# Strip attention: maxima and exponentials of two heads in one instruction over two PSUM banks

## Chip, cores, metric

One NeuronCore of a Trainium2 chip runs the whole program in one launch. The metric is the device time in microseconds (us) of an execution; the median over several runs is compared.

## What is computed

The input is an image batch of shape (2, 96, 256, 256). One layer normalises it over channels, runs windowed attention, a convolutional MLP on the map, adds the result to the input, and ends with a quantised feed-forward. The part that the change touches is the attention over overlapping windows of 16 x 16 pixels, 14 apart:

```python
tok = crop.transpose(0, 2, 3, 4, 5, 1).reshape(b * n, ps * ps, c)
y = _layernorm(tok, norm1_w, norm1_b)
q = (y @ wq).reshape(b * n, ps * ps, HEADS, hd_q).transpose(0, 2, 1, 3)
k = (y @ wk).reshape(b * n, ps * ps, HEADS, hd_q).transpose(0, 2, 1, 3)
v = (y @ wv).reshape(b * n, ps * ps, HEADS, hd_v).transpose(0, 2, 1, 3)
scores = jnp.einsum('bhnd,bhmd->bhnm', q, k) / jnp.sqrt(jnp.float32(hd_q))
attn = jax.nn.softmax(scores, axis=-1)
out = jnp.einsum('bhnm,bhmd->bhnd', attn, v)
tok = out @ wproj + tok
```

There are 4 heads, 256 tokens a window, 16 query and 24 value channels a head, and 2 x 19 x 19 = 722 windows. Their outputs are added where windows overlap, with weights.

## The kernel before

Three stages run one after another: `norm_stage`, `attention_stage` and `map_stage`. Each writes its result to HBM. Only `attention_stage` is touched. It goes through 38 strips of 16 rows (19 per image), and through 19 windows in each strip. Here they are counted from zero, windows 0 to 18, and strips as first, second, ... in order of time: "strip 11" is the eleventh, and its window 0 begins at 1901.98 us of the trace. A window begins where its transposes (L652) begin.

Every engine has its own program for the stage, written out for the 19 windows of a strip (`body`), and a hardware loop that holds two strips. The order on each engine is the order of the code; engines wait for each other by semaphores that count. What TensorE does for window j, in this order:

- `maxima` (L652): two transposes that turn the row maxima NM of window j into a row, in bank 0 (`B_MT`). It waits for all maxima of window j (L679) and for the exponential of head 0 of window j - 1 (L681), which read bank 0.
- `scores` of window j + 1, heads 0 and 1 (L645), in bf16, into banks 4 and 5. They are only there for the row maxima.
- in 16 of the 19 windows a query/key product of 512 tokens of a strip (`queries_keys`, L624, which waits for Y from GpSimd) or a projection (`project`, L632, which waits for GpSimd's sums), by the tables `QK_STEP` and `OUT_STEP`. Windows 9, 11 and 13 have none.
- `scores_t` (L660): the transposed scores of all four heads of window j in fp32, into banks 0 to 3. It waits for VectorE's query row QF (L696) and for the exponentials of window j - 1.
- `scores` of window j + 1, heads 2 and 3 (L645), into the same banks 4 and 5 as heads 0 and 1; so it waits for the maxima of heads 0 and 1 of window j + 1 (L701).
- `weigh` (L668) for window j - 1 and `values` (L636) for window j + 1.

VectorE makes for window j the query row QF from the transposed maxima (`query_row`, L806), then the four row maxima of window j + 1 (`row_max`, L812), then what the tables put there: `residual` (L830), `queries16` (L797), the reciprocals and shares of the softmax sums (`shares`, L820 and L824) and `keys16` (L801). ScalarE makes `keep_qk` (L737), the four exponentials of window j (L759) into PROB, then copies the values (L741) and the output of window j - 1 (L749).

SP moves the keys to their own tensor (L386), gathers the softmax sums of a group of windows (L394), stores their reciprocals (L401) and spreads them back (L405). GpSimd weighs the group's outputs and adds them up (L543 to L559), and makes the next strip's normalised input Y (L496). `GROUPS` are the windows 0 to 4, 5 to 9, 10 to 14 and 15 to 18.

The banks are named in one line, and the two places where a pair of heads is handled are these:

```python
B_ST, B_S, B_MT, B_OV, B_CK = (0, 1, 2, 3), (4, 5, 4, 5), 0, 6, 7

for u in range(4):
    A.activation(PROB[:, par, u, :], P[:, B_ST[u], :], ACT.Exp, scale=DQ ** -0.5).then_inc(act_exp, 1)

for u in range(4):
    if u % 2 == 0:
        dve.wait_ge(pe_s, n(s, 2 * NPOS, 2 * j + u // 2 + 1))
    V_.tensor_reduce(NM[:, :, 32 * u + DQ], P[:, B_S[u], :].rearrange("p (a m) -> p a m", a=2),
                     axis=AX.X, op=ALU.max).then_inc(dve_max, 1)
```

Of the kernel before, what the change touches and what calls it, by code (L numbers as in the profile page):

```python
# [7 lines left out]
HEADS, DQ, DV = 4, 16, 24  # L8
MLP, FFN = 192, 384
PATCH, STEP = 16, 14  # L10
NPOS = 19
# [10 lines left out]
ALU, ACT, AX = mybir.AluOpType, mybir.ActivationFunctionType, mybir.AxisListType  # L22
# [231 lines left out]
def attention_stage(nc, xhat, rnorm, n1w, n1b, wq, wk, wv, wproj, ident, share, qrows, sums, x2map, nstrip=NSTRIP):  # L254

    ctx = ExitStack()
    with ctx:
        def sb(name, shape, dt=fp32):
            return ctx.enter_context(nc.sbuf_tensor(name, shape, dt))
# [28 lines left out]
        NM = sb("NM", [128, 2, 128])  # L288
        PROB = sb("PROB", [128, 2, 4, 2 * PT])
        P = ctx.enter_context(nc.psum_tensor("P1", [128, 8, 512], fp32))  # L290
        B_ST, B_S, B_MT, B_OV, B_CK = (0, 1, 2, 3), (4, 5, 4, 5), 0, 6, 7
# [16 lines left out]
        NWINS = nstrip * NPOS  # L308
# [299 lines left out]
        def _(pe):  # L608
# [40 lines left out]
            def maxima():  # L649

                for half in range(2):
                    m = T.transpose(P[:, B_MT, half * 128:half * 128 + 128], NM[:, half, :], IDN[:, :])  # L652
                m.then_inc(pe_mt, 1)
# [19 lines left out]
            def body(s, n, k, prev, follow):  # L673
                kept, outs = 2, -4
                for j in range(NPOS):
                    par = (s * NPOS + j) % 2
                    more = follow or j < LAST
                    nj = (j + 1) % NPOS
                    pe.wait_ge(dve_max, n(s, 4 * NPOS, 4 * j + 4))  # L679
                    if prev or j > 0:  # L680
                        pe.wait_ge(act_exp, n(s, 4 * NPOS, 4 * j - 3))  # L681
                    maxima()
                    if more:
                        pe.wait_ge(dve_kb, n(s, NCK, NCK * ((j + 1) // NPOS) + first_new(nj) + 1))
                        scores(nj, 0, 1)
                    for c, at in QK_STEP.items():
                        if at == j and (c > 1 or follow):
                            queries_keys(s + (c < 2), n, c, n(s, NCK, outs) if prev or outs > 0 else None)
                            kept += 1
                    for c, at in OUT_STEP.items():  # L690
                        if at == j and (c < 4 or prev):
                            project(s - (c > 3), n, c, n(s, NCK, kept), n(s, NCK, outs) if prev or outs > 0 else None)
                            outs += 1
                        elif at == j:
                            outs += 1
                    pe.wait_ge(dve_qf, n(s, NPOS, j + 1))  # L696
                    if prev or j > 0:
                        pe.wait_ge(act_exp, n(s, 4 * NPOS, 4 * j))
                    scores_t(j)
                    if more:  # L700
                        pe.wait_ge(dve_max, n(s, 4 * NPOS, 4 * j + 6))  # L701
                        scores(nj, 2, 3)
                    pe.wait_ge(act_v, n(s, NPOS, j + 1))
                    if prev or j > 1:
                        pe.wait_ge(act_os, n(s, NPOS, j - 1))
                    if prev or j > 0:
                        weigh(1 - par)
                    if more:
                        values(nj)
# [3 lines left out]
            queries_keys(0, n0, 1, None)  # L713
            pe.wait_ge(dve_kb, 1)
            scores(0, 0, 1)
            pe.wait_ge(dve_max, 2)
            scores(0, 2, 3)
            values(0)
            strips(pe, body)
            last = nstrip - 1  # L720
            pe.wait_ge(act_exp, 4 * NWINS)
            pe.wait_ge(act_os, NWINS - 1)
            pe.wait_ge(act_v, NWINS)
            weigh((NWINS - 1) % 2)
# [4 lines left out]
        def _(act):  # L729
            A = nc.scalar  # L730
# [20 lines left out]
            def body(s, n, k, prev, follow):  # L751
                for j in range(NPOS):
                    par = (s * NPOS + j) % 2
                    for c, at in QK_STEP.items():
                        if at == j and (c > 1 or follow):
                            keep_qk(s + (c < 2), n, c, not prev and c > 1)
                    act.wait_ge(pe_st, n(s, NPOS, j + 1))
                    for u in range(4):
                        A.activation(PROB[:, par, u, :], P[:, B_ST[u], :], ACT.Exp, scale=DQ ** -0.5).then_inc(act_exp, 1)  # L759
                    if follow or j < LAST:  # L760
                        keep_v(s, n, j + 1, 1 - par)
                    if prev and j == 0:
                        keep_o(s - 1, n, LAST, k is None and s == 1)
                    elif j > 0:
                        keep_o(s, n, j - 1, not prev)
# [9 lines left out]
        def _(dve):  # L775
            V_ = nc.vector
# [29 lines left out]
                V_.scalar_tensor_tensor(QF[:, :], QS[:, win(j)], MSK[:, 0:1], P[:, B_MT, 0:PT], ALU.mult, ALU.subtract).then_inc(dve_qf, 1)  # L806

            def row_max(s, n, j):
                for u in range(4):
                    if u % 2 == 0:  # L810
                        dve.wait_ge(pe_s, n(s, 2 * NPOS, 2 * j + u // 2 + 1))
                    V_.tensor_reduce(NM[:, :, 32 * u + DQ], P[:, B_S[u], :].rearrange("p (a m) -> p a m", a=2),  # L812
                                     axis=AX.X, op=ALU.max).then_inc(dve_max, 1)

            def shares(s, n, q, first):

# [850 lines left out]
```

## Time and profile before

| | |
|---|---|
| median of 3 runs | 9166.02 us (9153.25 to 9173.01) |
| profiled execution, its own time | 9185.78 us |
| its span, first to last instruction | 9184.0 us |
| TensorE busy (matmul) | 8035.3 us, 87% |
| VectorE busy | 5221.1 us, 57% |
| ScalarE busy | 4672.3 us, 51% |
| GpSimd busy | 2150.5 us, 23% |
| attention stage, by the windows' first and last transposes | about 957 to 4550 us |

Times of instructions come from the one profiled execution. Matmuls are pipelined and overlap in the records, so a busy TensorE isn't TensorE at its peak. In a row of the timeline, the first number is the start and the second the time to the end of the last of the xN instructions, all in us; what stands in brackets is how long the engine sat idle before it and what released it. PEld is TensorE's weight load, which runs ahead of the multiplications, so its wait alone is no idle time of the array.

### The profile page before, as it was taken

The page shows a single profiled execution, that of the slowest core. Times are in us where ns is not written, and L with a number is a line of the kernel's source. Part 1 is how long each engine was busy: PE and PEld are TensorE (multiplying, and loading weights), DVE is VectorE, ACT ScalarE, POOL GpSimd, SP SyncE. Part 2 cuts the span into 40 slices and gives each one's busy share as a digit, 9 for nine tenths or more (in the row PEclk, how much of TensorE's full clock was granted, in tenths as well). Part 3 has the DMA queues.
Part 4 walks back from the last instruction along what each step waited for, and adds up shares of the span by engine and source line. Part 5 has one row for each costly group of instructions (what it writes and reads, how often), then busy time and mean ns, then how long its engine had stood idle before and what let it go on. Part 6 is the DMA issues. An engine that isn't in the chain of part 4 may idle for free.

```text
span 9184.0 us, 208496 instructions
## 1 busy us (share of the span) xinstructions
PE 8035.3 (87%) x76932; PEld 4839.5 (53%) x76932; DVE 5221.1 (57%) x9929; ACT 4672.3 (51%) x8702; POOL 2150.5 (23%) x1712
## 2 busy tenths in 40 slices
PE   6776899999999999999858989989989888998998
PEld 3333444444444444444445566666666666666665
DVE  5565677777777777777633444444444444444444
ACT  2221555555555555555525555555555555555554
POOL 0000333333333333333301211212111121121111
PEclk8888899999999999999969999999999999999999
DMA  4333343333433334333251111111111111111110
GB/s 119 113 114 104 88 98 87 91 94 84 100 83 94 94 84 98 86 92 94 71 45 34 44 40 34 44 40 35 43 40 43 35 43 41 34 44 40 35 43 24
DMA packets 480819, 612.84 MB, mean 67 GB/s; under 512 B 173263, under 2 KB 415697, under 8 KB 455317
## 3 DMA queue, kind: packets, MB, share of 16 engines
q1 hardware_dynamic: 480260, 605.46, 26.8%
q8 instruction: 343, 5.62, 0.3%
q14 instruction: 216, 1.76, 0.1%
HBM read 395.81 MB, written 166.64 MB: 61 GB/s over the span
## 4 chain that ended last, share of the span: by engine, by line
PE 28%; DVE 9%; ACT 7%; issue 5%; SPq 1%; DVEq 0%; ACTq 0%; DMA 0%; POOLq 0%; POOL 0%
PE P L1285 6%; PE P L1151 5%; PE P L1298 5%; PE P L1206 4%; ACT H L1358 4%; DVE H L1522 3%; PE P L1159 3%; DVE H L1515 2%; PE P L1314 2%; DVE Z L1537 2%; PE P L1125 1%; ACT Z L1383 1%; ACT L1383 1%; ACT L1346 1%; SPq L991 1%
## 5 line engine op out<-in xcount | busy, mean ns | idle before, releaser
L812 DVE TENSOR_REDUCE NM<-P 128x2 f32<-128x512 f32 x2888 | 1858.6, 686 | 719.2 <-PE P L645 714.3
L759 ACT ACTIVATE PROB<-P 128x512 f32<-128x512 f32 x2888 | 1491.1, 603 | 1090.7 <-PE P L660 1090.7
L1206 PE MATMUL P<-FC,XN 97*126 97x192 f32 x5408 | 1101.1, 343 | 15.7 <-ACT Y L1368 14.8
L1206 PEld LDWEIGHTS P<-FC,XN 97*126 97x126 f32 x5408 | 944.3, 197 | 167.9 <-issue 77.9
L660 PE MATMUL P<-QF,KS 32*128 32x256 f32 x11552 | 869.5, 417 | 94.0 <-DVE QF L806 93.2
L660 PEld LDWEIGHTS P<-QF,KS 32*128 32x128 f32 x11552 | 544.5, 192 | 642.0 <-DVE QF L806 506.6
L496 POOL TENSOR_TENSOR Y<-XHS,RNS 96x512 f32<-96x512 f32 x304 | 600.7, 2007 | 931.9 <-DMA RNS<-rnorm 931.9
L1352 ACT ACTIVATE SQ<-Z 96x512 f32<-96x512 f32 x260 | 163.8, 630 | 1286.5 <-DVE Z L1502 1286.5
L668 PE MATMUL P<-PROB,V 128*32 128x256 f32 x11552 | 797.8, 395 | 2.4 <-ACT PROB L759 1.5
L1368 ACT ACTIVATE Y<-P 126x384 f32<-126x384 f32 x1352 | 705.9, 570 | 109.2 <-PE P L1206 103.6
L1092 POOL TENSOR_TENSOR T<-T,Y 96x512 f16 (+1 forms) x260 | 299.2, 1151 | 1722.7 <-DVE Y L1526 1722.7
L1096 POOL COPY Z<-T 1x2560 f32 (+1 forms) x52 | 237.0, 4558 | 1906.4 <-PE P L1151 1906.3
L1298 PE MATMUL P<-Y,WC 127*64 127x52 f32 x19968 | 627.4, 223 | 27.6 <-ACT Z L1383 27.6
L1298 PEld LDWEIGHTS P<-Y,WC 127*64 127x64 f32 x19968 | 601.2, 139 | 62.7 <-ACT Z L1383 34.0
L645 PE MATMUL P<-KB,QB 32*128 32x256 bf16 x5776 | 574.3, 277 | 58.4 <-DVE KB L801 43.2
L543 POOL TENSOR_TENSOR EDGE<-OS,RBC 128x160 f32<-128x160 f32 (+2 forms) x152 | 82.2, 541 | 2253.8 <-DMA RBC<-sums 2253.8
L1537 DVE TENSOR_TENSOR Z<-P,Z 96x400 f32<-96x400 f32 (+1 forms) x728 | 342.5, 532 | 432.8 <-PE P L1314 432.8
L1285 PE MATMUL P<-XN,FC 97*96 97x440 f32 x1248 | 548.3, 562 | 3.8 <-issue 3.2
L636 PEld LDWEIGHTS P<-WQKV,Y 97*128 97x128 f32 x2888 | 379.1, 191 | 304.9 <-issue 304.9
L1151 PE MATMUL P<-Z,FC 97*96 97x430 f32 (+1 forms) x1248 | 499.3, 529 | 41.8 <-DVE Z L1537 41.8
L636 PE MATMUL P<-WQKV,Y 97*128 97x128 f32 x2888 | 517.2, 302 | 0.0
L1358 ACT ACTIVATE H<-P 128x1536 f16<-128x1536 f32 x260 | 377.0, 1450 | 240.1 <-DVE H L1522 183.4
(141 smaller groups left out, 12209.9 us busy)
## 6 DMA issues: line engine op xcount, KB each, us to landing
RBC<-sums SPq DMA_DIRECT2D x456, 160.0 KB, 3.1
X<-x2map SPq DMA_DIRECT2D x52, 1344.0 KB, 8.4
XHS<-xhat SPq DMA_DIRECT2D x76, 768.0 KB, 6.4
RNS<-rnorm SPq DMA_DIRECT2D x38, 1536.0 KB, 9.2
x2map<-XHS SPq DMA_DIRECT2D x76, 768.0 KB
T<-in_x SPq DMA_DIRECT2D x52, 960.0 KB
out<-T SPq DMA_DIRECT2D x52, 960.0 KB, 4.9
X<-in_x SPq DMA_DIRECT2D x32, 1536.0 KB, 13.3
```

What stands on the lines that cost most here:

```text
L496: G.tensor_tensor(Y[0:C, x, :], XH[0:C, s % 2, :, x].rearrange("c r w -> c w r"), RN[:, :, x].rearrange("c r w -> c w r"), ALU.mult).then_ ...
L636: v = T.matmul(P[:, B_OV, PT + half * 128:PT + half * 128 + 128], yf[:, win(j, half * 128, half * 128 + 128)], WQKV[:, 128:256], start=Tru ...
L660: m = T.matmul(P[:, B_ST[h], half * PT:(half + 1) * PT], KS[hr, win(j, half * 128, half * 128 + 128)], QF[hr, :], start=True, stop=True)
L668: m = T.matmul(P[32 * h:32 * h + 32, B_OV, 0:PT], V[:, par, half, 32 * h:32 * h + 32], PROB[:, par, h, half * PT:(half + 1) * PT], start=( ...
L759: A.activation(PROB[:, par, u, :], P[:, B_ST[u], :], ACT.Exp, scale=DQ ** -0.5).then_inc(act_exp, 1)
L812: V_.tensor_reduce(NM[:, :, 32 * u + DQ], P[:, B_S[u], :].rearrange("p (a m) -> p a m", a=2), axis=AX.X, op=ALU.max).then_inc(dve_max, 1)
L1151: m = M.matmul(P[0:C, j % 2, 0:px.stop - px.start], FC2[0:C + 1 - half, half, :], Z[0:C + 1 - half, half, px], start=(half == 0), stop=(ha ...
L1206: m = M.matmul(P[0:KW, 5 + (r + 2) % 3, i * MLP:(i + 1) * MLP], xnf[:, RI * WX * w:RI * WX * w + KW], FC1[:, :], start=True, stop=True)
L1285: M.matmul(P[0:C, 6 + k % 2, 0:(x1 - x0) * RO], FC1[:, half * C:(half + 1) * C], XN[:, 2 + x0:2 + x1, 2:2 + RO], start=True, stop=True).th ...
L1298: m = M.matmul(P[64 * half:64 * half + 64, 2 * (q % 2) + i // GP, (i % GP) * NWIN:(i % GP + 1) * NWIN], WC[:, (half * C + c) * MW:(half * ...
L1358: A.activation(H16[:, :, :], P[:, 0:3, :], ACT.Copy).then_inc(act_h, 1)
L1368: A.activation(Y1[0:KW, :, 2 * r:2 * r + 2], P[0:KW, 5 + (r + 2) % 3, 0:2 * MLP].rearrange("p (w c) -> p c w", w=2), ACT.Gelu).then_inc(ac ...
```

## The change

One VectorE instruction takes the maxima of two heads (banks 4 and 5, 1024 elements a partition, four rows of 256), and one ScalarE instruction the exponentials of two heads (banks 0 and 1, then 2 and 3). The counts of the two semaphores are halved with them. The wait ahead of the transposes was for the exponential of head 0 of the window before, and is now for heads 0 and 1 together.

```diff
-                    pe.wait_ge(dve_max, n(s, 4 * NPOS, 4 * j + 4))
+                    pe.wait_ge(dve_max, n(s, 2 * NPOS, 2 * j + 2))
                     if prev or j > 0:
-                        pe.wait_ge(act_exp, n(s, 4 * NPOS, 4 * j - 3))
+                        pe.wait_ge(act_exp, n(s, 2 * NPOS, 2 * j - 1))
                     maxima()
...
                     if prev or j > 0:
-                        pe.wait_ge(act_exp, n(s, 4 * NPOS, 4 * j))
+                        pe.wait_ge(act_exp, n(s, 2 * NPOS, 2 * j))
                     scores_t(j)
                     if more:
-                        pe.wait_ge(dve_max, n(s, 4 * NPOS, 4 * j + 6))
+                        pe.wait_ge(dve_max, n(s, 2 * NPOS, 2 * j + 3))
                         scores(nj, 2, 3)
...
-                    for u in range(4):
-                        A.activation(PROB[:, par, u, :], P[:, B_ST[u], :], ACT.Exp, scale=DQ ** -0.5).then_inc(act_exp, 1)
+                    for u in (0, 2):
+                        A.activation(PROB[:, par, u:u + 2, :], P[:, B_ST[u]:B_ST[u] + 2, :], ACT.Exp, scale=DQ ** -0.5).then_inc(act_exp, 1)
...
-                for u in range(4):
-                    if u % 2 == 0:
-                        dve.wait_ge(pe_s, n(s, 2 * NPOS, 2 * j + u // 2 + 1))
-                    V_.tensor_reduce(NM[:, :, 32 * u + DQ], P[:, B_S[u], :].rearrange("p (a m) -> p a m", a=2),
-                                     axis=AX.X, op=ALU.max).then_inc(dve_max, 1)
+                for i in range(2):
+                    dve.wait_ge(pe_s, n(s, 2 * NPOS, 2 * j + i + 1))
+                    V_.tensor_reduce(NM[:, :, :].rearrange("p a (u d) -> p u a d", d=32)[:, 2 * i:2 * i + 2, :, DQ],
+                                     P[:, B_S[0]:B_S[0] + 2, :].rearrange("p u (a m) -> p u a m", a=2), axis=AX.X, op=ALU.max)\
+                      .then_inc(dve_max, 1)
```

The same halving stands in the waits before the first and after the last strip. Nothing changes place. On VectorE, around the shares of the sums of the first group (window 7; L820, L824 the shares, L806 the query row, L801 and L797 keys and queries to bf16), the order before is:

```order
L806 SCALAR_TENSOR_TENSOR QF<-QS,MSK,P 128x256
L812 TENSOR_REDUCE NM<-P 128x2 x4
L820 RECIPROCAL RSC<-RSC 128x40
L824 TENSOR_TENSOR RSC<-RSC,SH 128x40
L801 TENSOR_SCALAR KB<-KS,MSK 128x512
L806 SCALAR_TENSOR_TENSOR QF<-QS,MSK,P 128x256
L812 TENSOR_REDUCE NM<-P 128x2 x4
```

and of the changed kernel:

```order
L806 SCALAR_TENSOR_TENSOR QF<-QS,MSK,P 128x256
L811 TENSOR_REDUCE NM<-P 128x2x2 x2
L820 RECIPROCAL RSC<-RSC 128x40
L824 TENSOR_TENSOR RSC<-RSC,SH 128x40
L801 TENSOR_SCALAR KB<-KS,MSK 128x512
L806 SCALAR_TENSOR_TENSOR QF<-QS,MSK,P 128x256
L811 TENSOR_REDUCE NM<-P 128x2x2 x2
```

Two reductions stand where four stood, in the same place. On ScalarE, in two windows with a copy of queries and keys (L737) between them, before:

```order
L759 ACTIVATE PROB<-P 128x512 x4
L741 ACTIVATE V<-P 128x256
L749 ACTIVATE OS<-P 128x256
L737 ACTIVATE QS<-P 128x512
L759 ACTIVATE PROB<-P 128x512 x4
```

and of the changed kernel:

```order
L759 ACTIVATE PROB<-P 128x1024 x2
L741 ACTIVATE V<-P 128x256
L749 ACTIVATE OS<-P 128x256
L737 ACTIVATE QS<-P 128x512
L759 ACTIVATE PROB<-P 128x1024 x2
```

Two exponentials of twice the width stand where four stood. TensorE's order of matmuls is the same; its queue has one register instruction less a window (that of L681).

## Rows read from the trace of the kernel before

**Rows 1.** The page's head and its part 1: the span, and TensorE's busy time.
```profile
span 9184.0 us, 208496 instructions
...
PE 8035.3 (87%) x76932; PEld 4839.5 (53%) x76932; DVE 5221.1 (57%) x9929; ACT 4672.3 (51%) x8702; POOL 2150.5 (23%) x1712
```

**Rows 2.** Busy time by stage: stretch, length, engines, PEclk, DMA share, GB/s; attention stage.
```profile
957.00:4550.00 3593.00, 3315.68 (x34134) 1734.01 (x34132) 2681.54 (x4781) 2083.76 (x4597) 1293.52 (x1319) 0.97 0.37 90
```

**Rows 3.** Groups of instructions, 957 to 4550 us: busy us, mean ns, idle before.
```profile
L812 DVE TENSOR_REDUCE NM<-P 128x2 f32<-128x512 f32 x2864 | 1843.1, 686 | 711.6 <-PE P L645 706.8
L759 ACT ACTIVATE PROB<-P 128x512 f32<-128x512 f32 x2864 | 1478.8, 603 | 1081.8 <-PE P L660 1081.8
```

**Rows 4.** Waits, 957 to 4550 us: us in total, times, longest us.
```profile
PEld P L645 <- DVE NM L812: 122.0, 275, 0.5
...
PE P L624 <- POOL Y L496: 59.0, 36, 3.2
```

**Rows 5.** Timeline, all engines, strip 11, window 3.
```profile
1919.38 1.28 DVE L812 TENSOR_REDUCE NM<-P 128x2 f32<-128x512 f32 x2
...
1920.22 1.15 PE L660 MATMUL P<-QF,KS 32*128 32x256 f32 x16
...
1921.20 0.38 PE L645 MATMUL P<-KB,QB 32*128 32x256 bf16 x4
1921.44 2.07 ACT L759 ACTIVATE PROB<-P 128x512 f32<-128x512 f32 x4 [2.06 <-PE P L660]
...
1921.63 1.29 DVE L812 TENSOR_REDUCE NM<-P 128x2 f32<-128x512 f32 x2 [0.97 <-PE P L645]
...
1923.07 0.42 PE L652 MATMUL P<-IDN,NM 128*128 128x128 f32 x2
```

**Rows 6.** Timeline, strip 11, window 9: maxima pair and scores' load.
```profile
1947.81 1.28 DVE L812 TENSOR_REDUCE NM<-P 128x2 f32<-128x512 f32 x2
...
1949.14 0.11 PEld L645 LDWEIGHTS P<-KB,QB 32*128 32x128 bf16 x4 [0.46 <-DVE NM L812]
```

**Rows 7.** Groups of instructions by shape, from 4600 us on (the map stage).
```profile
L1537 DVE TENSOR_TENSOR Z<-P,Z 96x400 f32<-96x400 f32 x624 | 314.2, 563 | 432.8 <-PE P L1314 432.8
...
L1537 DVE TENSOR_TENSOR Z<-P,Z 96x200 f32<-96x200 f32 x104 | 32.5, 352 | 0.0
...
L1358 ACT ACTIVATE H<-P 128x1536 f16<-128x1536 f32 x260 | 377.0, 1450 | 240.1 <-DVE H L1522 183.4 <-PE P L1185 56.8
```

**Rows 8.** Timeline, strip 11, from window 6 to window 7.
```profile
1933.64 0.43 ACT L749 ACTIVATE OS<-P 128x256 f32<-128x256 f32 x1
...
1934.16 2.42 SPq L394 DMA_DIRECT2D RSC<-OS  x4
...
1937.83 0.40 DVE L820 RECIPROCAL RSC<-RSC 128x40 f32<-128x40 f32 x1 [0.33 <-DMA RSC<-OS]
...
1939.35 1.15 PE L660 MATMUL P<-QF,KS 32*128 32x256 f32 x16
...
1940.51 0.11 PEld L645 LDWEIGHTS P<-KB,QB 32*128 32x128 bf16 x4 [0.41 <-DVE NM L812]
```

**Rows 9.** Timeline, SP and TensorE, strip 11 up to window 15; then strip 14's window 15.
```profile
1953.85 2.41 SPq L386 DMA_DIRECT2D KS<-QS  x4
...
1961.09 0.36 SPq L401 DMA_DIRECT2D sums<-RSC  x1
...
1974.76 1.13 PE L624 MATMUL P<-Y,WQKV 97*128 97x512 f32 x2 [0.61 <-POOL Y L496]
...
2263.49 2.08 PE L624 MATMUL P<-Y,WQKV 97*128 97x512 f32 x2 [2.34 <-POOL Y L496]
```

**Rows 10.** Busy time by stretch, columns as in rows 2: strip 14's window 15; strip 11's.
```profile
2263.49:2270.31 6.82, 6.82 (x43) 3.18 (x44) 1.29 (x2) 2.66 (x5) 5.65 (x3) 0.55 0.09 20
1973.41:1978.66 5.25, 4.64 (x50) 2.48 (x49) 3.42 (x6) 3.22 (x8) 5.25 (x4) 1.00 0.05 11
```

More of the change, by code:

```diff
@@ L715, in _ @@
             scores(0, 0, 1)
-            pe.wait_ge(dve_max, 2)
+            pe.wait_ge(dve_max, 1)
             scores(0, 2, 3)
@@ L720, in _ @@
             last = nstrip - 1
-            pe.wait_ge(act_exp, 4 * NWINS)
+            pe.wait_ge(act_exp, 2 * NWINS)
             pe.wait_ge(act_os, NWINS - 1)
```

## Prediction

> **What bounds the kernel now.** I read the page's head first, then the busy time by stage, the groups of instructions and the waits of the attention stage, and last the timeline of single windows of its eleventh strip. The page gives one execution of 9184.0 us, with TensorE busy 87% [rows 1]. The attention stage runs from 957 to 4550 us: 3593 us for 722 windows, just under 5.0 us each, with TensorE busy 3315.68 us of it, 92%, VectorE 75% and ScalarE 58% [rows 2]. The change touches no other stage, so everything is decided in these 3593 us, and an instruction saved on VectorE or ScalarE counts only where TensorE waits for it.
>
> The maxima take 2864 instructions of 686 ns and the exponentials 2864 of 603 ns there [rows 3]. ScalarE waits for the transposed scores and never the other way round: the waits list no TensorE wait for the exponentials at all. For the maxima there is one: the weight load of the scores of heads 2 and 3 waits for the maxima of heads 0 and 1, since both pairs share banks 4 and 5. That happened 275 times, 122.0 us in all [rows 4], 7.2 of the 19 windows of a strip. It is counted from the end of the load before it, with multiplications still under way, so 122 us is no idle time; what it says is in how many windows the maxima release TensorE last.
>
> An ordinary window shows the other 12. In window 3 of strip 11 a projection (L632) stands ahead of the transposed scores (L660), which start at 1920.22; the first maxima pair, 1919.38 to 1920.66, is over long before TensorE has done them and goes on to the scores of heads 2 and 3 at 1921.20 [rows 5]. Nothing that VectorE does faster shows there. Window 9 has neither a projection nor a query/key product: the first pair runs 1947.81 to 1949.09 and the scores' load starts at 1949.14, having waited for it [rows 6]. Here 0.05 us after the maxima end TensorE goes on, and all that a pair saves moves the rest of the window.
>
> **The change, part by part.** *Maxima.* Before, a pair is two reductions, 1.28 us from the first start to the last end [rows 5, 6]. After, it is one of 1024 elements over two banks. No VectorE row here reads more than 512 fp32 elements of PSUM, so the price is bounded. Lower end: one instruction's fixed part is paid once. VectorE's additions take 563 ns for 400 elements and 352 ns for 200 [rows 7], 1.055 ns an element; 686 + 512 x 1.055 gives 1.226 us. That saves 0.06 us a pair. Upper end: nothing is shared and it costs 2 x 686 = 1.37 us, 0.09 more than now. I take 1.226, as two instructions already overlap all but 0.06 of that fixed part (2 x 0.686 against 1.28), and the four rows of 256 that the instruction reduces are the same rows as before.
>
> The Trainium skill (Perfetto Trace Analysis, Optimizing Scalar/DVE Operations) puts VectorE's overhead per instruction on PSUM at about 125 ns; by it a pair would save twice as much as the rows give, and every gain below would double. The rows show two reductions starting about 0.6 us apart where their elements take 0.54, so the trace bears out only 0.06.
>
> *Exponentials.* Four take 2.07 us from first start to last end, each 603 ns [rows 3, 5]. ScalarE's cost by width is on record over several banks: 1450 ns for 1536 elements [rows 7], so (1450 - 603) / 1024 = 0.827 ns an element, and 1024 elements take 1.026 us. Starts lie (2.07 - 0.603) / 3 = 0.49 us apart, 0.423 of it elements, so the second of the wide ones starts 0.91 after the first and ends at 1.94: 0.13 us earlier than now. The signal that heads 0 and 1 are done comes at 1.03, where the one for head 0 alone came at 0.60. The transposes (L652) wait for it, since they write bank 0. In window 3 the exponentials start at 1921.44, so it would come at 1922.47, while the second maxima pair, for which the transposes wait too, ends at 1922.92 and TensorE reaches them at 1923.07 [rows 5]. The later signal costs nothing, with 0.6 us to spare. Without that cover (exponentials that start 0.6 us later against the transposes) the price would be up to 0.43 us a window.
>
> The Trainium skill says in that same section that where ScalarE or VectorE is not saturated but causes bubbles elsewhere, breaking instructions up may let work be completed sooner. That speaks against this change. If it held for the first release, each window would pay 0.43 us, 310 us in all; the second maxima pair and the matmuls in between forbid it in the rows.
>
> *Who waits for a faster VectorE or ScalarE.* (a) The 275 windows: 275 x 0.06 = 16.5 us. (b) Places where VectorE reaches the query row (L806) late because other work stands before it. In window 7 the reciprocal of the sums waits 0.33 us for its DMA, and query row and maxima follow; the load of the scores then waits 0.41 us [rows 8]. The DMAs that gather those sums started at 1934.16, right after ScalarE's copy of the window's output ended at 1934.07; that copy started without a wait, so it stood behind the exponentials on its engine [rows 8]. So here ScalarE's 0.13 arrives as well; TensorE's own work lets the scores come at most 0.18 earlier than now (they need 0.98 after the transposed scores start, as 1920.22 to 1921.20 shows [rows 5]; those start after the projection, at 1939.35 [rows 8]). Windows 13 and 17 have a residual and other copies between the last pair and the query row, and save two pairs, 0.12. Per strip that is 0.12 in window 7 beyond (a), 0.06 in 13, 0.06 in 17: 0.24 x 38 = 9 us. (c) One register instruction less a window on TensorE's queue, at nothing: loads are issued ahead of the array.
>
> All local gains: 16.5 + 9 = about 26 us.
>
> *What is given back.* TensorE also waits at gates whose time is set by a chain through SP, DMA and GpSimd. The longest: the query/key product of window 15 waits for Y, 36 times in the stage [rows 4]. In strip 11 the keys' DMAs go out at 1953.85, the shares of the sums at 1961.09, then GpSimd weighs a group and makes Y, and TensorE starts the product at 1974.76, idle 0.61 us before it [rows 9]. Those 21 us hold DMA and GpSimd time and little that gets faster. What windows 11, 12 and 13 save (0.06 + 0.06 + 0.12) only makes that idle time longer. The same holds behind window 17's share of the sums up to the keys of the next strip (0.06), and in window 2. Kept are 0.18 (window 7), 0.06 (window 9) and 0.06 (window 17, before its share): 0.30 a strip, 38 x 0.30 = 11 us. Against the profiled execution's 9185.8 us that is 9175; that execution lies 20 us above the median of the three runs, 9166.0, from which the forecast goes: 9155 us.
>
> **The rivals.** *Nothing is given back.* Gates that wait a little in one strip do not bind in the next, and chains start earlier too. Then all 26 us stay: 9140. For it: the gate idles only 0.61 us in strip 11. Against: 36 of 38 strips wait there.
>
> *The clock (slower).* A gain in front of a gate makes TensorE's idle time longer, and a long one costs clock. In strip 14 the product at 2263.49 had 2.34 us of idle time before it [rows 9], and the 6.82 us from there ran at a granted clock of 0.55 of 2.4 GHz, mostly the lower level of 1.2 GHz [rows 10]. From the product to the end of the window is 6.82 us there and 3.90 in strip 11 (1974.76 [rows 9] to 1978.66), where the clock was 1.00 [rows 10]: the fall costs 2.9 us. The stage's clock is 0.97 [rows 2]. If 0.24 us more at the gate brings 10 more of the 38 strips to fall, that is 29 us against the 11 kept: 9184. It decides from seven more falls on; below four the forecast stands.
>
> *Wide instructions don't share their fixed part (slower).* At 1.37 us a pair, 0.09 lost where 0.06 was gained, half of it kept: about 9183.
>
> *The change does not do what it says.* Excluded: the order of instructions has half as many, of 1024 elements.
>
> **How the numbers follow.** The forecast has 0.45, nothing given back 0.34, the clock 0.14, dear wide instructions 0.07. 0.2%, about what a measurement of this kernel can tell from no change, is 18 us: faster is below 9148, slower above 9184. Faster gets the second case and a little of the first, 0.37; slower most of the last two, 0.17; within 0.2% the rest, 0.46. The range reaches down to 9125 (all 26 us and a few falls of the clock fewer, 15 us) and up to 9190 (both slow cases at their size and a little over).
>
> **What would show it.** Right: reductions of about 1.23 us and exponentials of 1.03; waits of the scores' load for the maxima still some 275, in windows 7, 9, 11 to 13 and 17; window 9 shorter by 0.06; ordinary windows such as 3 as long as now; the wait for Y at window 15 longer by about 0.2. Wrong: transposes released by the exponentials; reductions over 1.29 us; the stage's clock off 0.97 by 0.01 or more; or the wait for Y unchanged with the stage 26 us shorter.

## The result, and the profile after

The changed kernel takes 9098.8 us, median of 7 runs (9092.17 to 9130.6), and the kernel before on the same chip 9169.55 (7 runs, 9151.93 to 9180.89): a ratio of 0.9932 with a 95% interval of [0.9914, 0.9949], so 0.68% less time. The forecast was 9155, no change that can be told, with a range down to 9125. Its profiled execution took 9125.05 us and has a span of 9123.2, against 9185.78 and 9184.0. TensorE's count of matmuls is the same as in [rows 1].

The head and part 1 of the page of the changed kernel:

```profile
span 9123.2 us, 205608 instructions
...
PE 7986.3 (88%) x76932; PEld 4808.5 (53%) x76932; DVE 5142.9 (56%) x8485; ACT 4583.1 (50%) x7258; POOL 2147.9 (24%) x1712
```

From its first to its last transposes the attention stage takes 3557.5 us, where it took 3618.9: all of the difference of the span, 61 us, is there. The busy time by stage, columns as in [rows 2], of the kernel before over the whole stage:

```profile
946.00:4566.00 3620.00, 3340.70 (x34357) 1747.29 (x34356) 2699.26 (x4813) 2098.96 (x4629) 1298.18 (x1322) 0.97 0.37 90
```

and of the changed kernel:

```profile
948.00:4506.00 3558.00, 3292.99 (x34355) 1719.70 (x34356) 2620.80 (x3370) 2009.15 (x3186) 1295.67 (x1322) 0.97 0.38 91
```

VectorE saves 78 us and ScalarE 90, TensorE is done 62 us earlier. Shown to two digits the clock stays at 0.97, but the time that the trace has below full speed in the stage falls from 229 us in 46 stretches to 184 in 43. Single executions scatter widely in this: over all runs shown below, kernels as slow as before have 181 to 253 us of it (`before_k127` 181), the faster ones 133 to 198.

The groups of instructions and the waits of the changed kernel's stage, 948 to 4506 us (columns as in [rows 3, 4]):

```profile
L811 DVE TENSOR_REDUCE NM<-P 128x4 f32<-128x1024 f32 x1443 | 1764.1, 1223 | 709.3 <-PE P L645 704.7
L759 ACT ACTIVATE PROB<-P 128x1024 f32<-128x1024 f32 x1442 | 1398.2, 1021 | 1117.8 <-PE P L660 1117.8
...
PEld P L645 <- DVE NM L811: 103.9, 277, 0.4
...
PE P L624 <- POOL Y L496: 36.0, 34, 3.0
```

A reduction is 1.223 us (forecast 1.226) and an exponential 1.021 (1.026). The maxima release the scores' load 277 times (forecast about 275), with 122.0 - 103.9 = 18.1 us less waiting, 0.065 a time (forecast 0.06). So each of these pieces came as reckoned. What did not: the wait of TensorE for Y was to grow by 0.2 us a strip, and it fell from 59.0 us [rows 4] to 36.0.

The timeline of the changed kernel in windows 3 and 9 of strip 11:

```profile
1898.40 1.15 PE L660 MATMUL P<-QF,KS 32*128 32x256 f32 x16
...
1899.38 0.38 PE L645 MATMUL P<-KB,QB 32*128 32x256 bf16 x4
...
1899.62 1.94 ACT L759 ACTIVATE PROB<-P 128x1024 f32<-128x1024 f32 x2 [2.02 <-PE P L660]
...
1899.81 1.23 DVE L811 TENSOR_REDUCE NM<-P 128x4 f32<-128x1024 f32 x1 [1.03 <-PE P L645]
...
1901.25 0.39 PE L652 MATMUL P<-IDN,NM 128*128 128x128 f32 x2
...
1927.35 1.22 DVE L811 TENSOR_REDUCE NM<-P 128x4 f32<-128x1024 f32 x1
1928.62 0.11 PEld L645 LDWEIGHTS P<-KB,QB 32*128 32x128 bf16 x4 [0.39 <-DVE NM L811]
```

The first exponential ends at about 1900.64, the second maxima at 1901.04, the transposes start at 1901.25: the later signal of the exponentials costs nothing, as forecast. From the scores of heads 2 and 3 to the next transposes it is still 1.87 us, as in [rows 5]. But the two transposes now end after 0.39 us and no longer after 0.42.

Where the time went shows only when the lengths of all windows are put side by side. Mean length in us over strips 3 to 36, from transposes to transposes. A hardware loop holds two strips, an even one and then an odd one, and the two differ; in what follows, "first strips" are the odd ones and "second strips" the even ones, counted in order of time:

| | before | after | difference |
|---|---|---|---|
| window 3 (median) | 4.545 | 4.510 | -0.035 |
| window 9 (median) | 4.063 | 3.965 | -0.098 |
| window 1, first strips | 6.025 | 6.716 | +0.69 |
| window 7, first strips | 4.854 | 5.378 | +0.52 |
| window 15, first strips | 5.948 | 5.982 | +0.03 |
| window 15, second strips | 8.963 | 5.663 | -3.30 |
| whole first strip | 94.93 | 95.87 | +0.94 |
| whole second strip | 96.65 | 92.51 | -4.14 |

One window of every second strip makes 3.30 x 19 = 63 us, the size of the whole gain. It is the window whose product waits for Y. Windows 1 and 7 of first strips, longer here, aren't longer in every execution: `after_again`, a second profile of the same changed kernel, has 6.24 us in window 1 and 4.83 in window 7, so +0.22 and -0.03 against before, and 5.41 in window 15 of second strips. Strip 12's window 15 is an example. TensorE in the kernel before:

```profile
2069.63 0.41 PE L652 MATMUL P<-IDN,NM 128*128 128x128 f32 x2
...
2073.11 1.13 PE L624 MATMUL P<-Y,WQKV 97*128 97x512 f32 x2 [2.74 <-POOL Y L496]
```

and in the changed kernel:

```profile
2045.31 0.38 PE L652 MATMUL P<-IDN,NM 128*128 128x128 f32 x2
...
2047.07 1.13 PE L624 MATMUL P<-Y,WQKV 97*128 97x512 f32 x2 [1.06 <-POOL Y L496]
```

Idle time falls by 1.7 us. Window 15 of strip 14, next, has in the kernel before (busy time by stretch, columns as above) 9.90 us at a granted clock of 0.66 of 2.4 GHz, part of it at the lower level of 1.2 GHz:

```profile
2260.41:2270.31 9.90, 7.56 (x51) 3.47 (x50) 3.42 (x6) 3.65 (x8) 8.55 (x6) 0.66 0.06 13
```

and in the changed kernel 5.74 us at full clock:

```profile
2230.51:2236.25 5.74, 4.60 (x50) 2.44 (x49) 3.22 (x4) 3.08 (x6) 5.74 (x4) 1.00 0.04 9
```

Followed back from Y: GpSimd begins its weighing (L543) once the spread shares (L405) have landed, and SP issues those once the store of the shares (L401) has landed. SP and GpSimd before, strip 12:

```profile
2057.30 0.37 SPq L401 DMA_DIRECT2D sums<-RSC  x1
2059.70 1.73 SPq L405 DMA_DIRECT2D RBC<-sums  x4
...
2066.28 0.52 POOL L543 TENSOR_TENSOR EDGE<-OS,RBC 128x160 f32<-128x160 f32 x1 [18.25 <-DMA RBC<-sums]
```

and after:

```profile
2033.21 0.37 SPq L401 DMA_DIRECT2D sums<-RSC  x1
2034.77 1.73 SPq L405 DMA_DIRECT2D RBC<-sums  x4
...
2040.18 0.53 POOL L543 TENSOR_TENSOR EDGE<-OS,RBC 128x160 f32<-128x160 f32 x1 [15.19 <-DMA RBC<-sums]
```

From the store to the spreading it was 2.40 us and is 1.56; from the spreading to GpSimd 6.58 and is 5.41. Neither has an instruction of VectorE or ScalarE in it. The DMA view names what differs. Before, from the store on (2057.3 to 2060 us), with the last row giving KB and us to landing:

```profile
q1 hardware_dynamic: 144, 0.02, 4.4%
q14 instruction: 1, 0.01, 0.8%
...
sums<-RSC SPq DMA_DIRECT2D x1, 20.0 KB, 2.3
```

After, 2033.2 to 2035.9 us:

```profile
q1 hardware_dynamic: 144, 0.02, 4.4%
...
sums<-RSC SPq DMA_DIRECT2D x1, 20.0 KB, 1.5
```

A single packet of queue 14, a piece of an engine's own program, falls into the store's flight before, and none after. In the kernel before this queue has eleven 8 KB packets in the 415 instructions that VectorE's loop over two strips has. Three of them stand 126 to 129 instructions of VectorE apart (counted in the order of its program against the packets' times), and these are the ones that move when VectorE's program alone is shifted (`before_k40`, below): they are VectorE's program, read from memory as it runs. Of the other eight, seven stand at the same counts in `before_k40`, so they don't belong to that sequence; whose they are was not tested. Of the store's 16 landings in strip 12, 15 are in by 2058.80 and the last comes at 2059.61.

**What the change did to that.** The two-strip loop of VectorE has 415 instructions before and 339 after, since 2 x 38 reductions are gone. Loads begin at its instructions 142, 268 and 397 before; 142 lies in window 12 of second strips. After, they begin at 54, 180 and 307, and none is in window 12. So the theory for the experiments was **(P)**, called F in the expectations: most of the gain is the place of VectorE's program load, and any edit that moves it gains the same, with no wide instruction. The rivals were **(W)**, called G there, the shorter durations of the wide maxima or the wide exponentials, and **(Q)**, TensorE's queue. The trace shows what became of that queue: the register instruction of L681 is gone, and an event instruction of the same line stands in the window instead, so that the queue holds as many instructions as before.

### The profile page after: what moved, and what is told of

Same layout as the page of the kernel before. It is cut to its first block, busy times and chain, and to the rows that moved or that the text cites. A ratio compares the mean times of both kernels' runs of the same rounds, so it can differ in the third digit from the quotient of the medians.

```text
span 9123.2 us, 205608 instructions
## 1 busy us (share of the span) xinstructions
PE 7986.3 (88%) x76932; PEld 4808.5 (53%) x76932; DVE 5142.9 (56%) x8485; ACT 4583.1 (50%) x7258; POOL 2147.9 (24%) x1712
## 3 DMA queue, kind: packets, MB, share of 16 engines
q8 instruction: 343, 5.62, 0.3%
q14 instruction: 196, 1.61, 0.1%
## 4 chain that ended last, share of the span: by engine, by line
PE 28%; DVE 9%; ACT 8%; issue 5%; SPq 1%; DVEq 0%; ACTq 0%; DMA 0%; POOLq 0%; POOL 0%
PE P L1285 6%; PE P L1151 5%; PE P L1298 5%; PE P L1206 4%; ACT H L1358 4%; DVE H L1522 3%; PE P L1159 3%; DVE H L1515 2%; PE P L1314 2%; DVE Z L1537 2%; PE P L1125 1%; ACT Z L1383 1%; ACT L1383 1%; ACT L1346 1%; SPq L991 1%
## 5 line engine op out<-in xcount | busy, mean ns | idle before, releaser
L811 DVE TENSOR_REDUCE NM<-P 128x4 f32<-128x1024 f32 x1444 | 1765.4, 1223 | 710.0 <-PE P L645 705.4
L759 ACT ACTIVATE PROB<-P 128x1024 f32<-128x1024 f32 x1444 | 1400.1, 1021 | 1119.4 <-PE P L660 1119.4
L543 POOL TENSOR_TENSOR EDGE<-OS,RBC 128x160 f32<-128x160 f32 (+2 forms) x152 | 80.6, 530 | 2194.5 <-DMA RBC<-sums 2194.5
```

The costliest lines, as they stand in the source:

```text
L759: A.activation(PROB[:, par, u:u + 2, :], P[:, B_ST[u]:B_ST[u] + 2, :], ACT.Exp, scale=DQ ** -0.5).then_inc(act_exp, 1)
L811: V_.tensor_reduce(NM[:, :, :].rearrange("p a (u d) -> p u a d", d=32)[:, 2 * i:2 * i + 2, :, DQ], P[:, B_S[0]:B_S[0] + 2, :].rearrange("p ...
```

## Experiments

### First four: which part of the change

`none_q` has TensorE's program of the changed kernel, but four maxima and four exponentials, of which every second one signals:

```diff
-                    for u in (0, 2):
-                        A.activation(PROB[:, par, u:u + 2, :], P[:, B_ST[u]:B_ST[u] + 2, :], ACT.Exp, scale=DQ ** -0.5).then_inc(act_exp, 1)
+                    for u in range(4):
+                        e = A.activation(PROB[:, par, u, :], P[:, B_ST[u], :], ACT.Exp, scale=DQ ** -0.5)
+                        if u % 2:
+                            e.then_inc(act_exp, 1)
```

and the same for the maxima. `max_q` is the changed kernel with only the exponentials undone so, `exp_q` with only the maxima. `after_oldq` is the changed kernel with the waits of before on TensorE:

```diff
-                      .then_inc(dve_max, 1)
+                      .then_inc(dve_max, 2)
```

and likewise for the exponentials.

> Four maxima and four exponentials as before, each second one signalling, so that TensorE's queue is that of the changed kernel: one register instruction less a window, the one that stood between the values and the transposes. Theory Q (this queue instruction costs 33 ns in each of the 722 windows, 24 us): 9145 to 9155 us, 15 to 24 us under before, and windows without any other wait 0.033 us shorter. Theory G (the gain comes from the wide instructions' shorter durations alone): no change, 9165 to 9175. Theory F (most of the gain comes from where the instruction loads fall, which moves with the length of every engine's program): anything between 9090 and 9190, with the wait of window 15 in every second strip changed.

> Wide maxima, four exponentials, TensorE's queue as in the changed kernel. Theory G: some 11 to 17 us faster than none_q, since 275 windows wait for the maxima and each saves 0.06 us. Theory Q alone: as none_q. Theory F: if the 8 KB instruction load that falls into window 12 of every second strip was VectorE's, it is gone here, the wait for Y at window 15 there falls by nearly 2 us or more, and the time falls to 9100 to 9120; if it was ScalarE's it is still there.

> Wide exponentials, four maxima, TensorE's queue as in the changed kernel. Theory G: 0 to 5 us faster than none_q. Theory F: if the instruction load of window 12 was ScalarE's, it is gone here and the time falls to 9100 to 9120.

> The changed kernel with TensorE's queue of before (signals count by two, so that the wait ahead of the transposes needs its own register instruction again). Theory Q: 15 to 24 us over the changed kernel, 9115 to 9125 us, with every ordinary window 0.033 us longer again. Theory G: as the changed kernel, 9099.

Measured against the kernel before (9176.24 us, 29 runs):

| | us | ratio | stage, us | window 3 |
|---|---|---|---|---|
| none_q | 9183.93 | 1.0002 [0.9987, 1.0017] | 3606.8 | 4.510 |
| max_q | 9111.16 | 0.9926 [0.9907, 0.9944] | 3550.8 | |
| exp_q | 9169.49 | 0.9991 [0.998, 1.0002] | 3615.6 | |
| after_oldq | 9171.89 | 0.999 [0.9977, 1.0003] | 3624.3 | 4.549 |

Two things seem plain, the first of them wrong: that the wide maxima are the whole gain (`max_q` has it, `exp_q` does not), and that TensorE's queue is needed too (`after_oldq`, both wide, has nothing). Yet the queue alone, in `none_q`, is worth nothing. An increment by 2 takes an instruction of its own, an event instruction for each of the 1442 reductions in the stage: VectorE's loop has 415 instructions in `after_oldq`, as before, and not 339, and its second maxima pair starts 0.07 us later in a window 3. So this run is no clean test of the queue; it is one of the length of the program, and its window 12 has the load again. That is why theory Q's 9115 to 9125 us did not come. All four agree with (P): `max_q` is the one of them with VectorE's short loop, and the only one that is faster than before.

### The place of the load alone

Forty increments of a semaphore that nobody waits for, ahead of VectorE's attention program, run once and do no work. They shift where in its loop each piece of program ends:

```diff
+            for _ in range(40):
+                dve.sem_inc(spare, 1)
```

`before_k40` is the kernel before with these 40. 128 of them are about one whole piece, so `before_k128` has the same additions and more, and the load back where it was. `after_k64` puts 64 into the changed kernel, to bring a load to window 12. `e_max` has wide maxima and four exponentials that all signal, so that TensorE has the register instruction of L681 again, and another at L698, where the kernel before has an event instruction.

> The kernel before, with 40 semaphore increments more on VectorE ahead of the strips, where it waits for weights: they only move its program by 40 instructions against the 8 KB pieces in which it is loaded, so that no piece is loaded in window 12 of every second strip (instruction 142 of the loop) but at 102, 228 and 357. Theory F (that load delays the last landing of the sums' store and of their spreading, and so Y and window 15): the stage gets shorter by 40 to 70 us, 9105 to 9135 us, window 15 of those strips 2 to 3 us shorter. Theory G (durations of the wide reductions) and theory Q (TensorE's queue): no change, 9170.

> Control: 128 increments, one whole piece, so that the loads fall where they fell before. Theory F: as the kernel before, within its noise, the load in window 12 still there. If padding as such did something, it would show here as in before_k40.

> The changed kernel with 64 increments ahead of the strips, which brings a load back to about instruction 117 of its loop, in window 12 of every second strip. Theory F: most of the gain is lost, 9145 to 9170 us, window 15 of those strips 2 to 3 us longer. Theories G and Q: as the changed kernel, 9099.

> Wide maxima and four exponentials, each signalling, so that TensorE's queue has two register instructions a window more than in max_q (one ahead of the transposes, one ahead of the transposed scores); VectorE's program is that of the changed kernel, its loads too. Theory F: fast, 9100 to 9130. Theory Q within the fast placement: 10 to 24 us slower than max_q's 9111, windows 3, 14, 16 longer by 0.033 us. If the queue costs nothing on the whole: as max_q.

Measured against the kernel before (9179.18 us, 17 runs):

| | us | ratio | stage, us |
|---|---|---|---|
| before_k40 | 9128.06 | 0.9951 [0.9937, 0.9966] | 3552.6 |
| before_k128 | 9172.64 | 0.9988 [0.9974, 1.0002] | 3640.9 |
| after_k64 | 9106.27 | 0.9922 [0.9909, 0.9936] | |
| e_max | 9121.74 | 0.9941 [0.9927, 0.9955] | 3572.6 |

With 40 idle instructions and no other edit the kernel before gains 0.49%, some 45 us; window 15 of second strips takes 5.29 us for 8.96, more than the 2 to 3 us expected. With 128 it takes 8.80 and nothing is gained. The same rows in `before_k40`, SP, GpSimd and TensorE of strip 12:

```profile
2032.86 0.37 SPq L401 DMA_DIRECT2D sums<-RSC  x1
2034.44 1.73 SPq L405 DMA_DIRECT2D RBC<-sums  x4
...
2039.65 0.53 POOL L543 TENSOR_TENSOR EDGE<-OS,RBC 128x160 f32<-128x160 f32 x1 [16.31 <-DMA RBC<-sums]
...
2046.55 1.13 PE L624 MATMUL P<-Y,WQKV 97*128 97x512 f32 x2 [0.62 <-POOL Y L496]
```

The store reaches the spreading in 1.58 us, GpSimd begins 5.21 later, TensorE idles 0.62 instead of 2.74. Its waits view of the stage, 947 to 4500 us:

```profile
PEld P L645 <- DVE NM L814: 121.0, 271, 0.5
...
PE P L624 <- POOL Y L496: 31.7, 35, 2.1
```

The wait for the maxima is that of before (122.0), the one for Y that of the changed kernel or less: the two parts of the gain, apart. `after_k64` missed. The gain stayed, because the load did not come to window 12 at all: the trace has five packets of queue 14 in a two-strip loop where the changed kernel has ten. The five stand in the changed kernel's loop too, and none of them is one of its three at 54, 180 and 307. Reckoned in pieces of 128, the 339 instructions of the loop cross two borders now and not three; why that spares every load was not tested. Part 3 of its page:

```profile
q14 instruction: 111, 0.91, 0.0%
```

against 196 packets in the changed kernel. `e_max` gains 0.59%, as the wide maxima and the moved load should. It lies above `max_q` (0.9926), but the intervals overlap, and theory Q's sign for it failed: windows 3, 14 and 16 were to be 0.033 us longer, and their median is the 4.510 us of `max_q`, with both register instructions in the queue. So no run shows a price for them once the maxima are wide.

### Wide instructions with the load out of the way

`none_k40` and `exp_k40` are `none_q` and `exp_q` with the same 40 increments, so neither has the load in window 12. `after_k22` puts 22 into the changed kernel, to bring a load to window 12 of first strips. `after_again` is the changed kernel itself, without an edit.

> None of the wide instructions, TensorE's queue of the changed kernel, VectorE's loads moved as in before_k40. Theory Q, with the load out of the way: 10 to 24 us faster than before_k40's ratio of 0.9951, that is 0.9925 to 0.994. If the gates take it all: 0.995.

> As none_k40, with wide exponentials. Theory G for the exponentials: within 5 us of none_k40, ScalarE having slack everywhere but at the copy before the first gather. It would be slower only if the later first signal held up the transposes, up to 0.43 us a window.

> The changed kernel with 22 increments ahead of the strips. Its loop of 339 VectorE instructions then has loads at about 32, 158 and 285, the last in window 12 of every other (first) strip, where the changed kernel has none. Theory F: window 15 of those strips 1.5 to 3.5 us longer, the kernel 30 to 60 us slower than the changed one, 9130 to 9160 us. Theory G: as the changed kernel.

> The changed kernel on the same chip, for comparison: 0.992 to 0.994. Theory G: what it is faster than none_k40 is the worth of the wide maxima and exponentials alone, 5 to 20 us.

Measured against the kernel before (9178.02 us, 17 runs):

| | us | ratio | stage, us |
|---|---|---|---|
| none_k40 | 9125.26 | 0.9942 [0.9924, 0.9961] | 3566.6 |
| exp_k40 | 9120.31 | 0.9943 [0.9924, 0.9962] | 3558.5 |
| after_k22 | 9102.01 | 0.9918 [0.99, 0.9935] | |
| after_again | 9096.89 | 0.9916 [0.9896, 0.9937] | 3533.4 |

The exponentials can't be told from nothing (0.9943 against 0.9942; `exp_q` against `none_q` is 0.11% with overlapping intervals). They do shorten window 7 by 0.12 us, from 4.766 to 4.642 in the median of `none_q` and `exp_q`, some 5 us over 38 strips by estimate. TensorE's queue without the register instruction isn't to be told from nothing either (0.9942 against 0.9951 of `before_k40`). The wide maxima are what is left: 0.9942 to `max_q`'s 0.9926 or the changed kernel's 0.9932 and 0.9916, so 0.10 to 0.26%, 9 to 24 us. That is a difference of ratios whose intervals overlap; what supports it is that single windows show it: window 9 is 4.063 us before, 4.031 in `none_q` and 3.965 in `max_q` and `e_max` (medians). `after_k22` missed: it lost nothing. Its load did come to window 12 of first strips, as the DMA view from such a store on (1933.9 to 1936.6 us) shows:

```profile
q14 instruction: 1, 0.01, 1.1%
...
sums<-RSC SPq DMA_DIRECT2D x1, 20.0 KB, 1.9
```

but the load began 1.13 us after the store was issued, and the store landed in 1.9 us, not in 2.3. So the place of the load within the flight matters, not the window alone.

### How near the load must come

`after_k24` has 24 increments in the changed kernel, so the load should begin two instructions of VectorE sooner against the store than in `after_k22`. `before_k127` has one less than the control `before_k128`.

> The changed kernel with 24 increments ahead, two more than after_k22: the load in window 12 of the other strips comes two VectorE instructions earlier, within 1 us of the store. If the overlap decides: from the store to the spreading 2.4 us or more in those strips, where after_k22 has 1.88 in the mean, window 15 there 0.5 to 0.9 us longer, the kernel 5 to 20 us slower than after_k22. If not: as after_k22, 0.992.

> The kernel before with 127 increments ahead, one less than the control: the load of window 12 comes one VectorE instruction later than before, some 0.5 us or more, beyond the store's landing. If the overlap with the store decides: the time from the store to the spreading falls from 2.44 to 1.57 us in every second strip, and the kernel is as fast as before_k40, ratio 0.993 to 0.997. If a load in that window costs as such: as the control, 0.9988.

Measured against the kernel before (9168.98 us, 17 runs): `after_k24` 9115.48 us, 0.9938 [0.9914, 0.9961]; `before_k127` 9172.88, 1.0004 [0.9986, 1.0023], stage 3597.9 us. In `after_k24` the load begins 1.04 us after the store, in `after_k22` 1.13; the DMA view of its store, 1938.9 to 1941.6 us:

```profile
q14 instruction: 1, 0.01, 1.2%
...
sums<-RSC SPq DMA_DIRECT2D x1, 20.0 KB, 2.5
```

It lands in 2.5 us, the time from store to spreading is 2.505 us in first strips against 1.88 in `after_k22`, and window 15 of first strips takes 7.33 us against 6.43. That is 0.9 us in 19 strips, 17 us, and between the ratios 0.20%, 18 us, were lost: of the right size, though the ratios' intervals overlap. What separates the two kernels is two idle instructions. `before_k127` missed its expectation of an escape: one instruction moves the load by only 0.03 us, to 0.996 to 1.04 us after the store, still in the harmful stretch, with 2.48 us from store to spreading.

Over strips 3 to 36 of the 16 traces, the time from window 12's store to the spreading, by when a load begins against the store's issue. Queue 8 carries 16 KB packets, 17 in a two-strip loop, and is taken for TensorE's by their number; no run moved it:

| load begins | strips | median, ns | range |
|---|---|---|---|
| none from 0.7 before to 1.7 us after | 292 | 1571 | 1560 to 1759 |
| VectorE's, 0.80 to 1.05 us after | 103 | 2433 | 2393 to 2662 |
| VectorE's, 1.05 to 1.3 us after | 17 | mixed | 1565 to 2696 |
| TensorE's (queue 8), 0.3 us before to 0 | 52 | 2049 | |
| TensorE's, 0 to 0.4 us after | 31 | 2365 | |

All six kernels at the time of before (before, `none_q`, `exp_q`, `after_oldq`, `before_k128`, `before_k127`) have VectorE's load 0.96 to 1.26 us after the store in 18 of 19 second strips; none of the faster ones has a packet of queue 14 there in more than one of them.

## Why the prediction was wrong

- **Maxima.** Right: 1.223 us an instruction, 0.06 saved a pair, 277 waits, 18.1 us less waiting. Windows 13 and 17 save the two pairs, 0.13 us (medians of second strips 4.362 to 4.231 and 4.845 to 4.717), and window 7 saves 0.16 of the 0.18 us. The runs with the load out of the way give the wide maxima 9 to 24 us, where the forecast kept 11 of 26. How much of what they save is given back at the gates was not isolated.
- **Exponentials.** Right: 1.94 us in all, first signal hidden, no transposes released by them, 0.12 us in window 7, and no gain on the whole that `exp_k40` could show.
- **Ordinary windows, "as long as now", and step (c) at nothing.** Wrong locally, and small in the sum: windows 3 are 0.035 us shorter. The text held that nothing that VectorE does faster shows there. But in strip 11 before, the second maxima pair ends at 1922.92, the register instruction of L681 follows at 1922.96, the first load of the transposes 0.085 us behind that, and the second transpose comes 0.143 us after the first. In `none_q` and `exp_q` the register instruction is gone, in `e_max` it stands but the wide maxima end 0.06 us earlier; in all three the second transpose comes after 0.113 us and window 3 takes 4.510 us. Either of the two is enough, and together they give no more. 722 x 0.033 is 24 us, but `none_q` is no faster than before: given back at the gates, as far as the runs can tell.
- **The step that failed is "What is given back":** the change was costed in durations and waits alone, and the chain to Y was taken as fixed, as 21 us that "hold DMA and GpSimd time and little that gets faster". That put at nothing what removing 76 instructions from VectorE's loop does: it moves the loads of its program, and one of them lay upon the 20 KB store in that chain. From the store to the product that waits for Y it is 15.4 us in second strips before and 13.8 in the changed kernel (means). `before_k40` shows it alone, with no wide instruction: 0.49%, against the 0.68% measured. The maxima's 0.10 to 0.26%, though not clear of noise, would make up the rest.
- **The given-back argument** is right in form (a later or earlier arrival only changes the idle time at the gate), but its sign was turned: the gate itself came 1.6 us sooner, counted from the store, in half the strips. The sign "the wait for Y unchanged with the stage 26 us shorter" was among what would show the forecast wrong; the wait in fact fell by 23 us in the profile, and the stage by 61.
- **The clock.** The rival had gains in front of a gate bring more falls. The opposite came: with the gate open sooner the falls got fewer, 229 to 184 us of low clock, though single executions scatter by more than that. Its "decides from seven more falls on" doesn't follow from its own numbers: seven falls of 2.9 us less the 11 kept are 9 us more than before, 9175, still within 0.2%; ten are needed. Of what window 15 gains, idle time is a part and clock the rest: in strip 14 it is 4.16 us shorter (9.90 to 5.74), of which 1.20 is idle time (2.34 [rows 9] to 1.14) and 2.96 the clock, the 2.9 that the text had for one fall.
- **The two places that name the Trainium skill (Perfetto Trace Analysis, Optimizing Scalar/DVE Operations).** With its 125 ns for an instruction's overhead on PSUM a pair would have saved about twice 0.06 us by estimate; the saving measured is 0.06. It says that breaking instructions up may let work be completed sooner; here the split exponentials, whose price was put at up to 0.43 us a window, showed no effect (0.9942 against 0.9943).

What stays open: why the five packets of `after_k64` are all that is left, what the other packets of queue 14 and those of queue 8 cost (in the table the spreading is issued 2.0 to 2.4 us after the store where a 16 KB packet begins beside it), and the worth of the wide maxima to better than 9 to 24 us. No run was clearly better than the changed kernel: `after_k22` (0.9918) and `after_k64` (0.9922, no load in the loop) lie within the intervals of `after` and `after_again` (0.9932, 0.9916).

## What to carry to other kernels

An edit that changes how many instructions an engine runs in a loop also moves where its program is loaded, and in a kernel with small DMAs in a gated chain that can be worth more than the edit: here 45 us against some 9 to 24. Before believing in a gain, or a loss, from merged instructions, run the kernel before with some idle instructions ahead of the loop and a control with one whole piece of them. And compare window by window, first and second strip of a loop apart: a mean over all 722 windows would have spread the 3.3 us of one window over everything.

## What the runs showed of the hardware that was not expected

- VectorE's program arrives in 8 KB packets, one every 126 to 129 instructions in the loop. They go through queue 14, most of whose packets don't stand in that sequence (196 in all, 1.61 MB, in the changed kernel; in a loop three of ten do). Queue 8 has 16 KB packets (343, 5.62 MB), by their number TensorE's. The Trainium skill (Runtime: NRT & Kernel Launch, Instruction fetch mechanics) says that an engine's sequencer fetches its program by a DMA queue of its own in blocks of 16 KiB, and that the cost of crossing a block is mostly hidden. For queue 8 the trace agrees in size, for VectorE it is 8 KB, and seven of the queue's packets in a loop stayed in place when VectorE's program was shifted (`before_k40`), which doesn't look like a queue of its own. That the loads cost the fetching engine little fits `after_k64`, which has none of VectorE's in its loop and is no faster than the changed kernel (0.9922 against 0.9932); for another engine's small DMA the cost isn't hidden.
- A single 8 KB load that begins 0.80 to 1.05 us after the store's issue delays the store's last landing: 2433 ns to the next issue instead of 1571, 0.86 us. 0.1 us later it may miss (`after_k22`, 1.13 us: 1.88 us in the mean). In strip 12 before, 15 of the store's 16 landings came by 2058.80 and the last at 2059.61: one part of the transfer alone is held up.
- A delayed transfer is moved onto the next collision. The spreading, issued 0.87 us late, then takes 6.16 instead of 5.3 us until GpSimd begins. In those strips it meets TensorE's 16 KB load, which begins about 5.5 us after the store in both cases. That this is the cause of the second 0.8 us was not isolated, but `after_k24` speaks for it: in its first strips the spreading is as late (2.5 us after the store), no packet of queue 8 begins in the 2 to 8 us after the store, and GpSimd begins 5.3 us after the spreading.
- A loop of 339 VectorE instructions can run without any load of its program (`after_k64`: 111 packets in queue 14 for 196). That bought nothing measurable here.
- A signal that counts by two isn't free: the increment by 2 on the maxima brings VectorE's loop from 339 to 415 instructions (`after_oldq`), one event instruction for each reduction.
- A wait that TensorE's queue holds on a register instruction right ahead of a weight load leaves 0.085 us between that instruction and the load (strip 11, window 3, before and in `e_max`).
